# Fourth block, second Gelu layer, first slice: the second Gelu on ScalarE becomes a cast on VectorE

## The reference

```
x = x + layernorm(attention(layernorm(x), W_qkv))
h = layernorm(x)
h = silu((h @ w1) * s1) * ((h @ w2) * s2)
h = gelu((h @ h1) * sh1)
h = gelu((h @ h2) * sh2)
x = x + layernorm((h @ w3) * s3)
```

## Time and profile before

| what | value |
|---|---|
| median of 3 runs | 134.16 us (134.15 to 134.47) |
| the profiled execution's own time | 134.64 us |
| its span, first to last instruction | 132.8 us |
| PE busy | 125.0 us, 94% of the span |
| DVE busy | 104.5 us, 79% |
| ACT busy | 99.2 us, 75% |
| POOL busy | 28.3 us, 21% |

### The profile page before, as it was taken

The page is one execution under the profiler, slowest core; times in us unless marked ns, Lnnn a source line. Parts: engine busy times, 40 slices in busy tenths (PEclk is TensorE's granted clock), DMA queues, the critical chain, the costliest instruction groups (busy, mean ns, idle before and its releaser), DMA issues. The chain is left out here.

```text
span 132.8 us, 2374 instructions
## 1 busy us (share of the span) xinstructions
PE 125.0 (94%) x699; PEld 102.8 (77%) x699; DVE 104.5 (79%) x355; ACT 99.2 (75%) x185; POOL 28.3 (21%) x39
## 2 busy tenths in 40 slices
PE   6999999999899999999999999999999999899970
PEld 4676968889787888787889888888786788689960
DVE  1777799999899999938799999386989954886433
ACT  3138878977999928399999085999983996996640
POOL 4281420035300023200100264300010430000352
PEclk9999999999999999999999999999999999999999
DMA  4899996000300000000000001020000011000002
GB/s 108 260 336 380 378 375 207 0 0 5 81 0 5 0 7 0 0 0 0 5 0 0 0 5 40 2 79 7 0 0 0 0 38 46 0 5 0 2 32 91
DMA packets 5344, 8.28 MB, mean 62 GB/s; under 512 B 464, under 2 KB 2768, under 8 KB 5328
## 3 DMA queue, kind: packets, MB, share of 16 engines
q1 hardware_dynamic: 3984, 5.19, 12.2%
q0 software_dynamic: 1344, 2.88, 6.8%
HBM read 7.02 MB, written 1.05 MB: 61 GB/s over the span
## 5 line engine op out<-in xcount | busy, mean ns | idle before, releaser
L307 POOL TENSOR_TENSOR rstd<-ve,minus_half 128x4 f32<-128x4 f32 (+1 forms) x19 | 18.5, 976 | 92.8 <-DVE ve L669 51.0
L1137 PE MATMUL F<-a_hi,h_hi 128*128 128x512 f32 (+1 forms) x160 | 37.7, 357 | 0.6 <-ACT act_full L417 0.6
L1143 PE MATMUL F<-a_lo,h_hi 128*128 128x512 f32 (+1 forms) x160 | 37.3, 353 | 0.1
L601 DVE TENSOR_TENSOR a_lo<-act_full,a_hi 128x512 fp32r<-128x512 f32 (+1 forms) x52 | 30.1, 604 | 4.5 <-ACT act_full L417 4.2
L425 ACT ACTIVATE a_hi<-F,sc 128x512 fp32r<-128x512 f32 (+1 forms) x36 | 21.9, 629 | 14.6 <-PE F L1143 14.5
L1143 PEld LDWEIGHTS F<-a_lo,h_hi 128*128 128x128 f32 x160 | 26.8, 188 | 5.4 <-DVE a_lo L601 1.1
L1137 PEld LDWEIGHTS F<-a_hi,h_hi 128*128 128x128 f32 x160 | 26.0, 188 | 5.0 <-ACT act_full L417 1.0
L417 ACT ACTIVATE act_full<-F,sc 128x512 f32<-128x512 f32 (+1 forms) x40 | 23.3, 620 | 1.0 <-PE F L1143 1.0
L699 DVE SCALAR_TENSOR_TENSOR act_full<-F,sc,silu 128x512 f32<-128x512 f32 (+1 forms) x16 | 10.7, 680 | 1.7 <-ACT silu L406 1.4
L1094 PE MATMUL F<-x2T_hi,w_hi 128*128 128x512 f32 (+1 forms) x32 | 10.3, 403 | 0.5 <-DVE x2T_lo L601 0.3
L406 ACT ACTIVATE silu<-F,sc 128x512 f32<-128x512 f32 (+1 forms) x16 | 9.8, 635 | 0.9 <-PE F L1097 0.7
(11 more groups left out here) (153 smaller groups left out, 194.7 us busy)
## 6 DMA issues: line engine op xcount, KB each, us to landing
h_raw<-h SPq DMA_DIRECT2D x2, 1024.0 KB, 11.5
h_hi<-h POOLq DMA_DIRECT2D x2, 1024.0 KB, 9.1
xs<-x SPq DMA_DIRECT2D x3, 256.0 KB, 3.7
out<-outs SPq DMA_DIRECT2D x3, 256.0 KB, 2.2
w_raw<-w SPq DMA_DIRECT2D x1, 512.0 KB, 6.7
w_hi<-w POOLq DMA_DIRECT2D x1, 512.0 KB, 7.5
xs<-x SPq DMA_DIRECT2D x2, 128.0 KB, 8.5
w_raw<-w SPq DMA_DIRECT2D x1, 256.0 KB, 15.4
```

The source lines that it names most:

```text
L307: nc.gpsimd.tensor_tensor(rstd[:, ln, tiles(b)], ve[:, ln, tiles(b)], minus_half[:, 0:SIZES[b]], ALU.pow).then_inc(rstd_ready[ln], 1)
L601: nc.vector.tensor_tensor(dst, full, hi.bitcast(f32), ALU.subtract).then_inc(done, 1)
L1137: nc.tensor.matmul(out, terms[k][0], terms[k][2], start=(k == 0), stop=False)
L1143: last = [nc.tensor.matmul(out, terms[k][0], terms[k][3], start=False, stop=(k == KT - 1)) for out, terms in groups]
```

## The change

ScalarE no longer issues `gelu_high(A3, 3, 0)`. In its place VectorE casts `act_full`, slice 0, to `a_hi`, between `shift_x1(4)` and `low(A3, 3, 0)`. The cast signals a semaphore of its own, `third_cast`, and the counts of `a_hi_ready[A3]` for the other slices of block 3 go down by one; `hi_done` gives semaphore and count for each slice, and VectorE's subtraction and TensorE's high pass wait by it. Everything else stays.

```diff
+        third_cast = sem("third_layer_cast")
...
+        CAST_SLICES = 1
+
+        def hi_done(n, b, o):
+            if n < A3 or b < LAST - 1:
+                return a_hi_ready[n], KT * b + o + 1
+            if o < CAST_SLICES:
+                return third_cast, o + 1
+            return a_hi_ready[A3], KT * b + o + 1 - CAST_SLICES
...
             silu(4, 3)
-            gelu_high(A3, 3, 0)
             gelu(A3, 3, 0)
             gelu_high(A3, 3, 1)
             gelu(A3, 3, 1)
...
                 dve.wait_ge(a_full[n], KT * b + o + 1)
-                nc.vector.tensor_copy(a_hi[n][:, o, c], full_of(n, b)[:, o, c]).then_inc(a_hi_ready[n], 1)
+                nc.vector.tensor_copy(a_hi[n][:, o, c], full_of(n, b)[:, o, c]).then_inc(hi_done(n, b, o)[0], 1)
...
-                lo_from(a_lo[n][:, o, c], full_of(n, b)[:, o, c], a_hi[n][:, o, c], a_hi_ready[n], KT * b + o + 1, a_lo_dve[n])
+                lo_from(a_lo[n][:, o, c], full_of(n, b)[:, o, c], a_hi[n][:, o, c], *hi_done(n, b, o), a_lo_dve[n])
...
             shift_x1(4)
+            high(A3, 3, 0)
             low(A3, 3, 0)
             low(A1, 4, 2)
...
                 for k in ks:
-                    pe.wait_ge(a_hi_ready[n], KT * b + k + 1)
+                    pe.wait_ge(*hi_done(n, b, k))
```

More of the change, by code:

```diff
@@ L317, in lo_part @@
                 c = slice(0, width(b))
-                pool.wait_ge(a_hi_ready[n], KT * b + o + 1)
+                pool.wait_ge(*hi_done(n, b, o))
                 pool.wait_ge(a_full[n], KT * b + o + 1)
```

## The result

Over 21 runs the changed kernel has a median of 133.98 us (133.44 to 135.1), and the kernel before, run beside it, 134.68 us (134.0 to 136.51). The ratio is 0.9955 with a 95% interval of 0.9938 to 0.9972: 0.45% faster, some 0.6 us, and by the interval between 0.38 and 0.83 us. (The quotient of the two medians is 0.9948, 0.70 us.) The forecast was -0.57 us, 0.43%. But it was tied to a level of 134.16 us, the median of three runs, and 21 runs put that level at 134.68. So the difference came out as forecast and the absolute time 0.39 us above it, at the upper edge of the range.

What follows compares the result with a forecast made beforehand. TensorE, busy for 94% of the span, was taken as the bound, with only its gaps to win: removed wait -0.57 us, cast 0, extra semaphore 0, downstream loss 0, from 134.16 to 133.59 us; range 133.3 to 134.0.

Steps and rivals of the forecast that it cites:

- The bound and the wait: TensorE bounds the kernel; its matmul-free hole from 115.74 to 116.35 us ends when ScalarE's gelu(A3, 3, 1) frees the bank.
- The size of the step: One Gelu of 128x512 less on ScalarE ahead of gelu(A3, 3, 1) lets TensorE restart 0.57 us earlier.
- The cast costs nothing: VectorE's added cast, step 0.52 us, fits into 0.43 us of idle time and the earlier Gelu; cost 0.
- What is late next: Inputs behind the hole have slack for TensorE's earlier arrival, nearest on VectorE low(A1, 4, 3) with 0.64 us; downstream loss 0.
- The outer bound: With no wait at all TensorE could restart at 115.58 instead of 116.35 us: at most 0.77 us gained.
- The level: The gain is taken off a median of 134.16 us, the profiled execution lying 0.48 us above it: 133.59 us.
- the partial case: Rival: ScalarE's stretch from 118.43 us does not move, y's transposes come 0.18 us later; gain 0.39, 133.77 us; chance 0.08.

Runs made afterwards that it cites:

- split_before: Kernel before, with TensorE's begin(A1, 4) cut in two so it waits for one bank at a time; stretch 21.08 us against 21.57, ratio 0.9941.
- extra_gelu: Kernel before, with one more Gelu of 128x512 on ScalarE between the two of slice 0; stretch 22.12 us against 21.57, ratio 1.0036.
- no_cast: Changed kernel without its cast, so the rounding of slice 0 is left out; stretch 20.95 us against 20.99, ratio to before 0.9953.
- one_more_cast: Changed kernel with one scratch cast of 128x512 more on VectorE behind low(A3, 3, 0); stretch 20.98 us against 20.99, ratio to before 0.99.
- two_slices: Changed kernel with slice 1 treated like slice 0, two Gelus less and two casts in all; stretch 20.99 us, ratio to before 0.9946.
- split_order: Changed kernel with begin(A1, 4) cut in two and VectorE's A1 steps ahead of the cast, shift_x1(4) behind the subtractions; stretch 20.70 us, ratio to before 0.9921.
- split_after: Changed kernel with TensorE's begin(A1, 4) cut in two, slice 0 and then slice 1; stretch 20.87 us against 20.99, ratio to before 0.995.
- order_only: Changed kernel with only VectorE's order changed, A1 steps ahead of the cast and shift_x1(4) behind the subtractions; stretch 20.96 us, ratio to before 0.9933.

## Why the prediction was right, and where not

**The bound and the wait.** Right. split_before, which changes nothing but the order in which TensorE asks for the two banks, closed the hole, and extra_gelu widened it by 0.56 us.

**The size of the step.** Right: 0.57 taken, 0.58 measured from mark to restart and from mark to end. The steps between starts are 0.58 and 0.57 in the changed kernel too. The price that the Trainium skill gives ("ScalarE: Activation LUTs", What ACT_TABLE_LOAD costs), 0.61 us by my estimate, was 0.04 too high for this stretch.

**The cast costs nothing.** Right, and shown by no_cast and one_more_cast. The subtraction started 6.40 us behind the mark instead of 6.38.

**What is late next.** Right for the changed kernel, where none of the listed inputs was waited for. The slack on VectorE was 0.55 instead of 0.64 us. The page of the Trainium skill with the rule to keep the number of Vector instructions low ("VectorE: DVE Perf Modes", Rules for kernel authors) does not bind while idle time stands ahead of the cast; in two_slices, where none did, one more cast cost what the closed hole had gained, 0.2 us.

**The outer bound.** Too low by a little. I gave 0.77 us from the hole alone; split_order reached 0.87. What was missing, for 0.08 of the 0.10 us, is what the wait costs behind its end: the six matmuls behind it take 0.80 us to the next start (116.35 to 117.15 before), and without a wait six take 0.72 (115.46 to 116.18 in two_slices).

**The level: the step that failed.** "The profiled execution lies 0.48 us above the median of 134.16; I take the same difference for the median: 133.59 us." The term that was mis-sized is the 134.16 from which the gain was taken off. It was the median of three runs, and by luck all three lay in the lower half: 134.15 and 134.16 are among the three fastest of the 21 runs of before, which include them. Over the 21 the level was 134.68, 0.52 us higher, nearly as much as the whole effect, and the profiled execution with its 134.64 had been an ordinary one. The forecast change on that level gives 134.68 - 0.57 = 134.11 us, against 133.98 measured. Sized by the two medians that a reader had in hand, 134.16 before and 133.98 after, the gain looks like 0.18 us, a third of what was forecast; against runs of before made beside it, it is 0.45%.

The range reached 0.41 us above the forecast, less than the error of the level. It holds the measured 133.98 by 0.02 us, thanks to the room left for the partial case, which did not occur: that is luck. And 21 runs don't fix the level for good either: in the three later groups the kernel before came to 134.74, 134.92 and 135.02.

## What to carry to other kernels

Where the bound engine waits for a PSUM bank, count the instructions that the other engine issues ahead of the one that frees it: each is worth its step until the wait is used up, and a step moved to an engine that idles right there costs nothing. The next limits are close together, so close the hole with the cheapest cut first and look at what then waits. For an effect of a few tenths of a per cent, compare a stretch from a mark to a mark in each trace, and take the level of the forecast from many runs or give it the width of their scatter.

## What the runs showed of the hardware

The start of this kernel scatters by up to 1.8 us between executions of nearly the same program, and it does so inside TensorE's instructions as well as in waits. The two matmuls of the g projection took 0.70 us in six traces, 0.84, 0.85 and 1.03 in four others, and 1.18 to 1.22 in three. The granted clock does not tell them apart: it reads 1.00, its upper level of 2.4 GHz, in that window before (the first row) and after (the second).

```profile
5.40:7.70 2.30, 2.18 (x14) 1.76 (x13) 2.20 (x14) 0.70 (x2) 0.72 (x1) 1.00 0.96 350
5.40:7.70 2.30, 2.30 (x10) 1.68 (x9) 2.19 (x15) 0.38 (x1) 0.73 (x1) 1.00 0.93 301
```

The mean clock of 0.992 in the trace of after does not come from here either: its windows are at 1.00 up to 130 us, and below it only behind the last matmul, at 0.78 and then 0.50, the lower level of 1.2 GHz. Two traces show other sources. In split_after the first weights landed 0.8 us later than in the others. In order_only the two matmuls took 0.70 us and started earlier than before, and yet its first scores of block 1 come 0.40 us later than before, because TensorE waited for a tile of VectorE, which itself had waited 1.11 us for the DMA that brings the scales:

```profile
10.38 1.10 PE L999 MATMUL A<-ident,xn_odd 128*128 128x128 f32 x4 [0.96 <-DVE xn_odd L627]
```

Before, TensorE's wait was 0.17 us. What makes the matmuls of the start long in one execution and short in the next was not tested and stays open.
